# A four-layer graph network on one core: one-hots made during the loads, weights loaded once in the preparation, and a gather that runs beside the making of its table

## The reference, cut to what matters

```python
# L0: two graph convolutions, then log_softmax
agg = segment_sum(x[src], dst);  h = relu(((1 + eps) * x + agg) @ wa + ba) @ wb + bb
# L1: embedding to 128 features, four rounds of an edge MLP and a node MLP, out_w
# L2: relational attention; weight and w_comp give one 16x16 matrix per relation
W_rel = einsum(w_comp, weight)            # 90 relations
y = x[src] @ W_rel[edge_type_90]          # a message per edge
gate = y @ a0 + x[dst] @ a1 + edge_attr_16 @ a2
out = segment_sum(gate * y, dst)
# L3: two relational convolutions over 8 edge types with means
```

## Time and profile before

| | |
|---|---|
| median of 3 runs | 8562.17 us (8555.83 to 8563.68) |
| profiled execution | 8550.26 us, of which 8548.6 us are the span of the core |
| TensorE busy | 6428.4 us (75%) |
| GpSimd busy | 5192.9 us (61%) |
| VectorE busy | 4918.4 us (58%) |
| ScalarE busy | 2820.3 us (33%) |
| bytes moved | 1000.54 MB, mean 117 GB/s |

### The profile page before, as it was taken

One profiled execution on the slowest core, in us unless ns is written; L12 is line 12 of the kernel. 1 busy time (PEld: TensorE's weight loads), 2 busy tenths in 40 slices (PEclk: granted clock), 3 DMA queues, 4 the chain that ended last, 5 costly groups with the idle time before them and its releaser, 6 DMA issues. The chain is left out here.

```text
span 8548.6 us, 233535 instructions
## 1 busy us (share of the span) xinstructions
PE 6428.4 (75%) x55142; PEld 5292.3 (62%) x55143; DVE 4918.4 (58%) x13561; ACT 2820.3 (33%) x8471; POOL 5192.9 (61%) x7408
## 2 busy tenths in 40 slices
PE   1222215767699998999899989997866666888998
PEld 1111113555477776888688868886455555887998
DVE  7333345867455655666466646664322223998999
ACT  1222212545333333333333333332133333222554
POOL 2777754756477766777577757774277775222554
PEclk8555556555599999999999999998555555999999
DMA  2000003434388886888688878885200001332232
GB/s 66 3 3 3 3 29 104 120 97 120 88 221 216 216 197 181 222 221 222 161 222 222 222 164 223 222 222 121 95 7 7 7 7 24 82 82 57 73 73 59
DMA packets 1319112, 1000.54 MB, mean 117 GB/s; under 512 B 479354, under 2 KB 1223183, under 8 KB 1318092
## 3 DMA queue, kind: packets, MB, share of 16 engines
q1 hardware_dynamic: 941322, 649.30, 27.7%
q0 software_dynamic: 134272, 178.98, 10.8%
q10 hardware_dynamic: 243392, 170.76, 6.9%
HBM read 951.88 MB, written 54.19 MB: 118 GB/s over the span
## 5 line engine op out<-in xcount | busy, mean ns | idle before, releaser
L1480 POOL DMA_INDIRECT qg<-q_tab,qidx x2520 | 2389.2, 948 | 940.1 <-issue 699.2
L1635 DVE COPY ps<-b 128x384 f32<-128x384 f32 x1120 | 628.0, 561 | 1381.2 <-ACT h L1600 1374.8
L1067 PE MATMUL ps<-rhs_i,ohi 128*128 128x128 f32 (+2 forms) x8640 | 1215.7, 266 | 210.1 <-issue 197.2
L1067 PEld LDWEIGHTS ps<-rhs_i,ohi 128*128 128x128 f32 (+1 forms) x8640 | 1000.4, 163 | 342.5 <-issue 282.0
L1033 POOL COPY near<-x 128x48 bf16 x2160 | 675.9, 351 | 789.4 <-PE ps L1056 434.0
L1195 POOL DMA_INDIRECT got_m<-y_tab,idx_m x832 | 815.8, 981 | 478.8 <-issue 251.4
L1549 PE MATMUL ps<-ohm,h 128*128 128x128 f32 x6720 | 1032.9, 290 | 65.3 <-DVE ps L1635 33.9
L1549 PEld LDWEIGHTS ps<-ohm,h 128*128 128x128 f32 x6720 | 838.8, 192 | 257.7 <-issue 242.8
L1593 ACT ACTIVATE h<-ps,b 128x384 f32<-128x384 f32 x1120 | 650.2, 581 | 1052.2 <-PE ps L1531 955.6
L375 POOL DMA_INDIRECT list_by_src<-ring,rpos x808 | 783.1, 969 | 349.0 <-issue 255.0
L1212 PE MATMUL ps<-rhs_m,ohi_m 128*128 x2880 | 668.1, 403 | 416.1 <-ACT rhs_m L1238 387.3
(11 more groups left out here) (442 smaller groups left out, 8623.6 us busy)
## 6 DMA issues: line engine op xcount, KB each, us to landing
pb<-p_tab ACTq DMA_DIRECT2D x1680, 96.0 KB
pb<-p_tab SPq DMA_DIRECT2D x1680, 96.0 KB
places<-place_by_turn SPq DMA_DIRECT2D x560, 192.0 KB
places_i<-place_by_meeting SPq DMA_DIRECT2D x360, 256.0 KB, 3.4
places_i<-place_by_meeting SPq DMA_DIRECT2D x720, 128.0 KB, 3.1
qb<-q_tab SPq DMA_DIRECT2D x840, 64.0 KB
qg<-q_tab,qidx POOLq DMA_INDIRECT x2520
nears<-near_by_turn SPq DMA_DIRECT2D x560, 64.0 KB
```

What stands on the lines that cost most here:

```text
L1067: m = pe.matmul(ps[:, bass.ds(to[j], width)], ohi[:, h, j, :], rhs[:, h, j, 0:width], start=False, stop=True, skip_group_check=True)
L1480: pool.indirect_dma_start(qg[:, h, j, :], None, q_tab, IndirectOffsetOnAxis(ap=qidx[:, h, j:j + 1], axis=0)).then_inc(m_got[h], 16)
```

## The change

It does the following.

1. **Start.** `ws` and `wa` are issued at once and have a semaphore of their own; `x` and `nodev` are issued behind them without waits between, and are first waited for at L0.
2. **Edge arrays.** The tail memsets have no waits between them; the one of `ea16` goes to GpSimd. SyncE starts after four memsets. VectorE waits for `srct` and `dstt` only, and then makes all of `ohs` (4 instructions of twice the size). ScalarE packs three parts of `rec` and does the multiplication of all four quarters of `ea16`, 16 instructions per quarter; GpSimd sums quarters 2 and 0, VectorE 3 and 1.
3. **Counting and scatter.** `ohs` is gone from here. VectorE clears a tile `blank`, and SyncE writes it over all of `y_tab` in 25 DMAs, each waited for. L2's `gg` is made here and saved to `g_tab`.
4. **Decode.** ScalarE's queue issues all weights of L0, L1 and L3 (43 DMAs) in the first block. VectorE makes one more row (`blk_i`), SyncE writes it to DRAM.
5. **Layers.** The `load` blocks ahead of L0, L1, L2 and L3 are gone. For L1, `maskT` and `b2` are still loaded, without a block of their own; the memset of `maskT` shrinks from 3200 to 75 columns. For L2, `wr` is loaded from `g_tab` beside the transposes.
6. **L2.** The making of `y_tab` moves into the block of `message_pass`, ahead of the sums on TensorE and VectorE. SyncE counts blocks that have landed in `y_ready`. ScalarE, before it writes the indices of a group, waits until the block of the group's last tile has landed (the first 8 rounds, 32 groups), and for all 25 blocks after that.

```diff
 # start, SyncE and VectorE
-                    sp.wait_ge(s_init, 1)
...
-                        sp_dma(sp, sp.dma_start(ws[:, :], a["L2_gnn_Ws"]), 16)
...
+                        sp.dma_start(ws[:, :], a["L2_gnn_Ws"]).then_inc(s_wsa, 16)
...
+                        sp.wait_ge(s_init, 1)
+                        sp.dma_start(x[:, 0:N // P, :], a["x"][0:full, :].rearrange("(b p) f -> p b f", p=P)).then_inc(s_x, 16)
...
-                    dve.wait_ge(sp_dma.sem, n_dma)
+                    dve.wait_ge(s_wsa, 32)
 # edge arrays
+                        pool.memset(ea16[P - 32:P, TAIL:T, :], 0.0).then_inc(s_tails16, 1)
...
-                        for q in (2, 3):
+                        for k, q in ((0, 2), (1, 0)):
                             lo, hi = q * TQ, (q + 1) * TQ
-                            pool.wait_ge(s_ea[q], 16 * len(by_edge(ea16, a["edge_attr_16"], lo, hi)))
-                            p_chain(pool, pool.tensor_tensor(ea16[:, lo:hi, :], ea16[:, lo:hi, :],
-                                                             a_rows[:, 0:1, :].to_broadcast([P, TQ, FIN]), ALU.mult))
+                            pool.wait_ge(s_times, k + 1)
...
-                        sp.wait_ge(s_pad, 1)
+                        sp.wait_ge(s_tails, 4)
...
+                        act.wait_ge(s_load, 2 * 3 * 16)
+                        act.activation(rec[:, :, 1], dstt[:, :], ACT.Copy).then_inc(s_pack, 1)
...
+                        for q in (2, 0, 3, 1):
...
+                            for f in range(FIN):
+                                m = act.activation(ea16[:, lo:hi, f], ea16[:, lo:hi, f], ACT.Copy, scale=a_rows[:, 0, f:f + 1])
+                            m.then_inc(s_times, 1)
...
-                        dve.wait_ge(s_load, 4 * 3 * 16)
+                        dve.wait_ge(s_load, 2 * 3 * 16)
...
+                        for j in range(J):
+                            dve.tensor_tensor(ohs[:, :, j, :], iota_b[:, None, :].to_broadcast([P, Q, KS]),
+                                              sbf[:, j * Q:(j + 1) * Q][:, :, None].to_broadcast([P, Q, KS]), ALU.is_equal)
 # counting and scatter, SyncE
+                    sp.wait_ge(blank_set, 1)
+                    for b in range(NB):
+                        sp.dma_start(y_tab[b * P * NREL:(b + 1) * P * NREL, :].rearrange("(p r) o -> p (r o)", p=P), blank[:, :]).then_inc(blank_out, 16)
+                        sp.wait_ge(blank_out, 16 * (b + 1))
...
-                            dve.tensor_tensor(ohs[:, lo:lo + HQ, j, :], iota_b[:, None, :].to_broadcast([P, HQ, KS]),
 # decode, ScalarE's queue
+                        for pairs, landed in ((w_of_l0, w0_in), (w_of_l1, w1_in), (w_of_l3, w3_in)):
+                            for d, s_ in pairs:
+                                act.dma_start(d, s_).then_inc(landed, 16)
 # L2, message_pass(xT, wr, yb)
+                        def landed(b):
+                            sp.wait_ge(y_out[b % 2], 16 * (b // 2 + 1))
+                            sp.sem_inc(y_ready, 1)
+
+                        for b in range(NB):
+                            sp.wait_ge(to_pe.sem, b_cp + 3 * b + 3)
+                            sp.dma_start(y_tab[b * P * NREL:(b + 1) * P * NREL, :].rearrange("(p r) o -> p (r o)", p=P),
+                                         yb[:, b % 2, :]).then_inc(y_out[b % 2], 16)
+                            if b >= 1:
+                                landed(b - 1)
+                        landed(NB - 1)
...
+                            if not isinstance(k, int) or k >= KY:
+                                act.wait_ge(y_ready, NB)
+                            else:
+                                last = (k * U + h) * G + G - 1
+                                of = address(mybir.EngineType.Activation, blk_at[0:1, last:last + 1], NB - 1)
+                                act.wait_ge(y_ready, (of[0] & 31) + 1)
                             act.activation(idx[:, h, :], rel_s[:, bass.ds((k * U + h) * G, G)], ACT.Copy).then_inc(d_idx, 1)
 # L3
-            load([(w1[:, :], a["L3_gnn_W1"].rearrange("r i o -> (r i) o")), (r1[:, :], a["L3_gnn_root1"]),
...
+                    dve.wait_ge(w3_in, 16 * len(w_of_l3))
```

More of the change, by code:

```diff
@@ L146, in by_edge @@
             return pairs
+        s_x = sem("s_x")
         with ExitStack() as st:
@@ L183, in _ @@
                     v_chain(dve, dve.memset(x[:, :, :], 0.0))
+                    dve.memset(nodev[:, :], 0.0).then_inc(s_init, 1)
                     v_chain(dve, dve.memset(nothing[:, :], 0.0))
@@ L186, in _ @@
                     v_chain(dve, dve.memset(ones16[:, :], 1.0))
-                    dve.memset(nodev[:, :], 0.0).then_inc(s_init, 1)
-                    dve.wait_ge(sp_dma.sem, n_dma)
+                    dve.wait_ge(s_wsa, 32)
                     v_chain(dve, dve.tensor_scalar(wab[:, 0, :], ones16[:, :], wa[:, 1:2], None, ALU.mult))
@@ L218, in gnn_kernel @@
             iota_b = sb("iota_b", [P, KS], BF16, st)
+            ohs = sb("ohs", [P, Q, J, KS], BF16, st)
             with ExitStack() as sa:
@@ L234, in gnn_kernel @@
                 s_col = sb("s_col", [P, 3], F32, sa)
-                s_pad, s_load, s_ew, s_fill, s_rows = sem("s_pad"), sem("s_load"), sem("s_ew"), sem("s_fill"), sem("s_rows")
+                s_pad, s_load, s_type, s_ew, s_fill, s_rows = (sem("s_" + n) for n in ("pad", "load", "type", "ew", "fill", "rows"))
+                s_tails, s_tails4, s_tails16 = (sem("s_" + n) for n in ("tails", "tails4", "tails16"))
+                s_pack, s_times = sem("s_pack"), sem("s_times")
                 s_ea = [sem(f"s_ea{q}") for q in range(4)]
@@ L343, in gnn_kernel @@
             identb = sb("identb", [P, P], BF16, st)
+            blank = sb("blank", [P, NREL * 17], F32, st)
+            blank_set, blank_out = sem("blank_set"), sem("blank_out")
+            wcT = sb("wcT", [NBAS, NREL], F32, st)
+            vv = sb("vv", [NBAS, 16, 16], F32, st)
+            gg = sb("gg", [NREL, 16, 16], F32, st)
+            g_in, g_mm, g_cp = sem("g_in"), sem("g_mm"), sem("g_cp")
             ring = sb("ring", [P, 2, 2 * J, W], F32, st)
             rpos = sb("rpos", [P, 2, 2 * J], I32, st)
-            s_ohs, s_ohd, s_cnt, s_evd, s_eva = (sem("s_" + n) for n in ("ohs", "ohd", "cnt", "evd", "eva"))
+            s_ohd, s_cnt, s_evd, s_eva = (sem("s_" + n) for n in ("ohd", "cnt", "evd", "eva"))
             s_sum, s_two = sem("s_sum"), sem("s_two")
@@ L395, in _ @@
                         m.then_inc(s_cnt, 1)
+                    pe.wait_ge(g_in, 32)
+                    pe.wait_ge(s_evd, 2 * len(CB))
+                    pe.wait_ge(s_eva, 2 * len(CB))
+                    pe.matmul(banks[4][0:NREL, 0:256], wcT[:, :], vv[:, :, :].rearrange("b i o -> b (i o)"), start=True, stop=True).then_inc(g_mm, 1)
                     pe.wait_ge(s_sum, 1)
@@ L479, in _ @@
                 def _(dve):
+                    dve.memset(blank[:, :], 0.0).then_inc(blank_set, 1)
                     v_chain(dve, dve.memset(upto[:, 0:1], 0.0))
@@ L593, in gnn_kernel @@
             blk_s = sb("blk_s", [1, NT], F32, st)
+            blk_i = sb("blk_i", [1, NT], I32, st)
+            b_blk = sem("b_blk")
             iv = sb("iv", [P, IC], F32, st)
@@ L643, in _ @@
                     sp.dma_start(meet_l2.rearrange("(p g) k -> p g k", p=P), l2_i[:, :, :]).then_inc(b_out, 16)
+                    sp.wait_ge(b_blk, 1)
+                    sp.dma_start(tile_block[:, :], blk_i[:, :]).then_inc(b_out, 16)
                     sp.wait_ge(b_plc, 3)
                     sp.dma_start(place_i[0, :].rearrange("(c i p) -> i c p", c=12, p=P), place_buf[0:IQ, :, :]).then_inc(b_out, 16)
-                    sp.wait_ge(b_out, 16 * 3)
+                    sp.wait_ge(b_out, 16 * 4)
+                @block.scalar
+                def _(act):
+                    with nc.allow_non_contiguous_dma(reason="small weights"):
+                        for pairs, landed in ((w_of_l0, w0_in), (w_of_l1, w1_in), (w_of_l3, w3_in)):
+                            for d, s_ in pairs:
+                                act.dma_start(d, s_).then_inc(landed, 16)
                 @block.tensor
@@ L1202, in _ @@
                             pe.matmul(banks[i], nothing[:, 0:P], nothing[:, :], start=True, stop=True)
+                        for b in range(NB):
+                            for c in range(3):
+                                n = 3 * b + c
+                                if n >= 6:
+                                    pe.wait_ge(to_pe.sem, b_cp + n - 5)
+                                pe.matmul(y_bank(n), xT[:, b * P:(b + 1) * P],
+                                          wr[:, :, :].rearrange("i r o -> i (r o)")[:, c * YC:(c + 1) * YC], start=True, stop=True).then_inc(from_pe.sem, 1)
                         pe.wait_ge(d_at, 16)
@@ L1705, in _ @@
                 def _(dve):
-                    v_chain(dve, dve.memset(maskT[:, :], 0.0))
+                    v_chain(dve, dve.memset(maskT[:, N:NP], 0.0))
```

247 lines of the change are left out of this document (123 added, 124 removed).

## The result

The changed kernel takes 8344.8 us (median, 8340.7 to 8350.6) beside 8562.9 for the kernel before (four runs; 8562.17 was the median of the first three): ratio 0.9745, 95% interval 0.9728 to 0.9762. The profiled execution has a span of 8339.0 us against 8548.6, a gain of 209.6 where the forecast had 186. Since nothing runs across the stages, the gain can be read as a lead: how much earlier the same event comes.

What follows compares the result with a forecast made beforehand. Bounds were read per stage: DMA in edge arrays, VectorE in counting, GpSimd's issue in scatter and L2 gathers. Terms 47 - 1 - 4 + 8 + 19 + 112 + 5 = 186 off 8562.2 gave 8376 us, range 8340 to 8412.

Steps and rivals of the forecast that it cites:

- Start, edge arrays and counting, 47: Stages before the scatter: earlier loads gain 20 us, one-hots leaving the counting gain 27; scatter starts 47 us earlier (42 to 52).
- Scatter, -1: Scatter: 25 blank-writing DMAs run beside it; the two-place ring leaves some 7 us of slack; cost 0 to 5, taken as 1.
- Decode, -4: Decode: 43 weight loads on ScalarE's queue come partly ahead of `lt`, `cum_row` and `v_row`; loses 4 us (0 to 8).
- Entry of L0, +8: Entry of L0: `from_at` and `to_at` still land behind the `rows_36` copies on SyncE's queue; gain 8 us (6 to 11).
- rival (c): Entry of L0: SyncE's queue doesn't hold `to_at`; gain 14 us there, time 8362 us; chance 0.06.
- the long middles are untouched: L1's four rounds and L3's both passes: the change touches only edges between stages and the order of L2's halves.
- L2, +112: L2: gathers start 133 us earlier, beside the table; catch-up costs 25, faster gathers give 4; gain 112 us (100 to 130).
- the lock: L2's catch-up: each gather meets the next `ohi` and takes 1.74 us a step instead of 1.284; 25 us lost.
- Rival (a): L2's catch-up: no lock, through a higher TensorE clock or uneven pace; L2 gives 133 us, time 8355; chance 0.17.
- rival (b): L2's table: its copies also lock gathers, so 90 gathers become 66; time 8400 us; chance 0.10.
- rival (d): L2: no overlap, `y_ready` releases the first group only near the table's end; time 8471 us; chance 0.06.
- Rival (e): L2: the lock never ends, all 742 gathers after the table take 1.74 us; time 8689, slower than before; chance 0.04.

Runs made afterwards that it cites:

- joined: Changed kernel with `ohi` built by four one-SBUF-tensor instructions, `rows_36` copies on ScalarE's queue, and the last `ea16` quarter multiplied by VectorE: 10492.5 us, slower chip.
- table_first_pad: Changed kernel with no index list before all 25 L2 table blocks are written, plus 32 unused TensorE matmuls beside the edge arrays: 8437.8 us.
- before_again: The kernel before, unedited, profiled a second time on the slower chip: 10661.5 us.

## Why the prediction was right or wrong

The time (8376) was 31 us too high and inside its range, 5 us above the lower end. Of the 31 us, 24 are the sum (209.6 us in the profile against 186). The other 8 come from taking the median 12 us above the profiled execution; for the changed kernel it is 4 above. Without L1's 20.7 us the sum would be right within 3 us. By its own steps:

**Start, edge arrays and counting, 47; measured 44.** The first `srct` issue came at 8.0 (7.6 forecast), the last quarter at 57.7 (57.5 forecast; seen in `joined`, on the slower chip). The step that failed is the one behind it: 16 instructions of at most 0.37 us behind the last load, after the row of a 256-column copy. They take 0.53 us each, 34 us for all 64, so ScalarE and not DMA is the bound, and the block ended at 73.3 instead of 70.5. Two rows of after point at how the elements lie in memory: `rec<-ew` writes one float in each 32 bytes, `rec<-ea` four in each 32.

```profile
25.94 1.65 ACT L288 ACTIVATE rec<-ew 128x808 f32<-128x808 f32 x1 [5.96 <-DMA ea<-in_edge_attr_dram]
27.39 3.62 ACT L289 ACTIVATE rec<-ea 128x3232 f32<-128x3232 f32 x1
```

That is 2.0 ns an element against 1.1; the 202 elements, one in each 64 bytes, take 2.6. The fight of VectorE and GpSimd was there and cost nothing.

**Scatter, -1; measured 0.** The slack of the ring hid 25 writes wholly. **Decode, -4; measured -3.3.** (1.0 to 1.3 MB at 307 GB/s are 3.3 to 4.2 us, not the 3.5 to 4.5 of the prediction.) **Entry of L0, +8; measured +7.4**, for the reason given: the queue's order, shown by moving the copies. That refutes rival (c). **Entry of L1, +19; measured +19.4. Entry of L3, +5; measured 5.3** (a wait of 0.53 us instead of 5.78):

```profile
7005.75 0.57 DVE L1244 CAST x<-x 128x400 bf16<-128x400 f32 x1 [0.53 <-PEq L2048]
```

**L1, 0; measured +20.7.** The premise that "the long middles are untouched" failed. It was true of the instructions and of the clock (0.97 to 0.98 over L1 in both), and false of the addresses. This is most of the 24 us by which the sum fell short. No row of before could show it; but the diff declares one more array ahead of four others, and that line was not costed.

**L2, +112; measured 115.5.** The first gather came 132.6 us earlier against the end of L1 (133 forecast) and 12.7 us behind the table's first matmul. The catch-up cost 17.1 us net where 21 stood in the sum. What failed is the size of the lock: the prediction made each gather of the catch-up 1.74 us "as long as the pace is even". It is uneven at every fourth group, which frees two gathers of five: 1.49 us instead of 1.74. It also makes the catch-up longer, 150 us instead of 116: in the cycle of 7.49 us five gathers bring 2.16 groups and TensorE does four, so 38 groups of backlog need some 155 us by this estimate. The two errors pull opposite ways, so that the cost came within 4 us is in part luck. Rival (a), no lock, is refuted by the timeline, and by the 43 us that the edit to `ohi` gave; rival (b), the copies of the table lock as well, by gathers of 0.94 us beside them; rival (d), no overlap, by `table_first_pad`. Rival (e), a lock that never ends, did not come: 84 gathers in 125 us leave TensorE time, and from 6200 us on the pace is that of before.

## What to carry to other kernels

A price taken from a row of the nearest shape (0.37 us for 256 columns) should come from the same access too: 202 elements, one in each 64 bytes, took 0.53, and 64 of them became the bound. Which of the differences counts (stride, element type, PSUM or SBUF) no run took apart; the two `rec` rows above point at the stride. When an engine's work is pushed back into a dense stretch, look at what its pace does to an engine that it can hold up, and write the small operand as a scalar for each partition where that avoids it. Four instructions of 0.28 us instead of one of 0.69 made L2 43 us shorter where the gathers were its bound, and some 40 longer where they were not. And a new array in device memory ahead of hot tables is an edit to them: compare a variant with the old order before a gain or a loss in an untouched stage is explained.

## What was not expected of the hardware

Moving L1's tables by one array of 3.3 KB changed the kernel by 16 us and back by 17 to 24, with TensorE's longest stops at the ends of L1's rounds at 6.7 to 11.7 us in the old place and at most 6.9 in the new.

What an `ohi` costs a gather is no fixed amount: all 133 gathers over 1.0 us end 0.81 to 0.83 us behind the end of the `ohi` in which they start, so the loss is what is left of the `ohi`, less some 0.12 us. One that starts in the last 0.12 us of it loses nothing.

A chip of the same type ran the same kernel in 10637 us instead of 8559. The page's rates (GB/s in 40 slices), of before where it takes 8550 us and of `before_again` on the slower one:

```profile
GB/s 66 3 3 3 3 29 104 120 97 120 88 221 216 216 197 181 222 221 222 161 222 222 222 164 223 222 222 121 95 7 7 7 7 24 82 82 57 73 73 59
```

```profile
GB/s 54 3 3 3 3 64 122 101 120 116 147 148 150 148 133 144 146 147 144 135 147 146 145 129 155 147 147 144 108 77 6 6 6 6 1 82 82 58 73 62
```

In L1 some 147 GB/s stand where 222 stood, while the median gather is 0.944 us in both. But transfers are not all of it. TensorE's granted clock in L1 is 0.84 there beside 0.97, and a matmul takes 0.31 us where it took 0.28. In L2, which moves 6 or 7 GB/s on either, TensorE stands for nothing that the profile shows (issue). The page's groups (busy us, mean ns, idle us before and what ended most of it), an L1 and the L2 matmul, in before and then in `before_again`:

```profile
L1540 PE MATMUL ps<-w,h 128*128 128x128 f32 x6720 | 939.1, 276 | 0.0
L1212 PE MATMUL ps<-rhs_m,ohi_m 128*128 x2880 | 668.1, 403 | 416.1 <-ACT rhs_m L1238 387.3
```

```profile
L1540 PE MATMUL ps<-w,h 128*128 128x128 f32 x6720 | 1106.1, 309 | 0.0
L1212 PE MATMUL ps<-rhs_m,ohi_m 128*128 x2880 | 691.2, 402 | 751.6 <-issue 658.7
```

What makes these stops stays open. Two edits have another sign or size there: building `ohi` by columns costs some 40 us instead of giving 43, and the overlap gives 79 instead of 101. What bounds a stage belongs to the chip as much as to the kernel.
